# A two-layer transformer kernel: a place in SBUF for every expert block's weights, loads issued from the last heads, clears in 23 pieces

## The reference, cut to what matters

```python
x = _layernorm(x + _L0_attn_ref(x, ...))   # 16 heads of 8, causal
x = _layernorm(x + _L0_ffn_ref(x, ...))    # 8 experts, top 2, 128 -> 256 -> 128, relu
x = _layernorm(x + _L1_attn_ref(x, ...))   # 16 heads of 8, causal, low-rank q and k
x = _layernorm(x + _L1_ffn_ref(x, ...))    # attention with 16 heads of 4, then 8 experts, top 2, gelu

def _L0_ffn_ref(x, Wr, br, W1, b1, W2, b2):
    logits = xf @ Wr + br
    topk_w, topk_idx = jax.lax.top_k(logits, TOP_K)
    topk_w = jax.nn.softmax(topk_w, axis=-1)
    gate = jnp.sum(jax.nn.one_hot(topk_idx, NUM_EXPERTS) * topk_w[..., None], axis=1)
    h = jax.nn.relu(jnp.einsum('th,ehf->etf', xf, W1) + b1[:, None, :])
    y = jnp.einsum('etf,efh->eth', h, W2) + b2[:, None, :]
    out = jnp.einsum('te,eth->th', gate, y)
```

## Time and profile before

| | |
|---|---|
| median of three runs | 1288.14 us (1286.03 to 1291.64) |
| the profiled execution | 1290.43 us, of which the span of the trace is 1288.6 us |
| PE busy | 1098.4 us, 85% |
| DVE, ACT, POOL busy | 69%, 58%, 26% |
| granted clock of PE, mean | 0.943 |
| stage 0's block units, stage 1's | from about 341 to 392 us, and 1162 to 1215 us |

### The profile page before, as it was taken

One profiled execution on the slowest core, in us unless ns is written; L12 is line 12 of the kernel. 1 busy time (PEld: TensorE's weight loads), 2 busy tenths in 40 slices (PEclk: granted clock), 3 DMA queues, 4 the chain that ended last, 5 costly groups with the idle time before them and its releaser, 6 DMA issues.

```text
span 1288.6 us, 25320 instructions
## 1 busy us (share of the span) xinstructions
PE 1098.4 (85%) x8672; PEld 598.6 (46%) x8672; DVE 883.8 (69%) x2110; ACT 742.8 (58%) x1535; POOL 338.9 (26%) x873
## 2 busy tenths in 40 slices
PE   5979999998659979999988998887888788866796
PEld 3456666554557645666645632212122211125675
DVE  2867767784213658888777888988998889801265
ACT  4456665566214425776656657777887667854232
POOL 8233322336204313433223310111110014200040
PEclk9899999999779979999999989999999989987898
DMA  3464333111342061234211311101111001033310
GB/s 89 116 184 105 99 91 94 36 39 52 105 125 64 19 161 39 62 94 104 74 59 41 69 34 25 25 11 27 34 34 33 17 15 32 18 90 103 93 40 25
DMA packets 73437, 83.04 MB, mean 64 GB/s; under 512 B 12406, under 2 KB 47430, under 8 KB 73054
## 3 DMA queue, kind: packets, MB, share of 16 engines
q1 hardware_dynamic: 71262, 77.22, 23.4%
q0 software_dynamic: 2048, 4.20, 1.1%
HBM read 47.98 MB, written 32.77 MB: 63 GB/s over the span
## 4 chain that ended last, share of the span: by engine, by line
PE 56%; DVE 23%; issue 7%; SPq 5%; ACT 5%; DMA 3%; POOL 1%; POOLq 0%; ACTq 0%; DVEq 0%
DVE tile_max L1132 17%; PE bank L1519 14%; PE bank L1475 11%; PE bank L1490 7%; PE bank L1688 6%; PE bank L1672 4%; ACT probs L1024 3%; PE bank L1470 3%; DMA q_parts<-x_blocks 2%; PE bank L1529 1%; PE bank L1596 1%; SPq L616 1%; SPq L617 1%; DVE tile_max L1126 1%; DVE x L1199 1%
## 5 line engine op out<-in xcount | busy, mean ns | idle before, releaser
L1024 ACT ACTIVATE probs<-bank 128x512 f32<-128x512 f32 x1088 | 576.3, 603 | 286.9 <-PE bank L1490 285.5
L1132 DVE TENSOR_REDUCE tile_max<-bank 128x1 f32<-128x512 f32 (+3 forms) x1152 | 611.8, 591 | 57.1 <-PE bank L1475 52.6
L1475 PE MATMUL bank<-qk 125*128 125x128 bf16 (+2 forms) x1664 | 397.1, 316 | 71.2 <-DVE tile_max L1132 66.6
L1490 PE MATMUL bank<-qk 128*128 128x128 bf16 (+1 forms) x1664 | 389.2, 311 | 3.9 <-ACT probs L1024 3.7
L1519 PE MATMUL bank<-probs,v_head 128*32 128x512 f32 (+3 forms) x3328 | 311.3, 463 | 0.8 <-POOL probs L877 0.7
L1475 PEld LDWEIGHTS bank<-qk 125*128 125x128 bf16 (+1 forms) x1664 | 135.4, 98 | 341.2 <-DVE tile_max L1132 258.1
L1519 PEld LDWEIGHTS bank<-probs,v_head 128*32 128x32 f32 x3328 | 142.4, 110 | 53.3 <-issue 28.0
L1490 PEld LDWEIGHTS bank<-qk 128*128 128x128 bf16 (+1 forms) x1664 | 135.6, 97 | 54.2 <-ACT probs L1024 17.1
L1126 DVE TENSOR_REDUCE tile_max<-bank 128x4 f32<-128x512 f32 x128 | 87.3, 687 | 98.1 <-PE bank L1475 97.7
L877 POOL TENSOR_SCALAR_AFFINE_SELECT probs<-probs 128x512 f32<-128x512 f32 x128 | 81.4, 636 | 141.1 <-ACT probs L1024 140.9
L845 POOL CAST neg_parts<-neg_max 128x8 bf16<-128x8 f32 x96 | 18.2, 189 | 327.1 <-DVE neg_max L1139 327.1
(11 more groups left out here) (175 smaller groups left out, 874.1 us busy)
## 6 DMA issues: line engine op xcount, KB each, us to landing
qk<-qk_parts SPq DMA_DIRECT2D x160, 144.0 KB
sb_w<-in_w SPq DMA_DIRECT2D x92, 128.0 KB, 2.5
qk_parts<-q_parts SPq DMA_DIRECT2D x48, 192.0 KB, 2.4
qk_parts<-k_parts SPq DMA_DIRECT2D x48, 192.0 KB, 3.0
x_blocks<-zeros SPq DMA_DIRECT2D x2, 1472.0 KB, 8.0
q_parts<-x_blocks SPq DMA_DIRECT2D x10, 256.0 KB, 3.5
y_blocks<-sums SPq DMA_DIRECT2D x10, 256.0 KB, 2.9
qk_parts<-q_parts SPq DMA_DIRECT2D x24, 96.0 KB, 2.3
```

The lines of the kernel that those rows point to most:

```text
L1024: nc.scalar.activation(probs[:, hd.probs_place(c), :], S2[i % len(S2)][:], ACT.Exp, scale=hd.a.scale).then_inc(sem("probs"), 1)
L1132: ins = nc.vector.tensor_reduce(tile_max[:, hd.slot, t, which:which + 1], s1[:, at:at + P * count], AX.X, ALU.max)
L1475: ins = mm(s1[:, at:at + P * count], qk[hd.query_rows, hd.place, 0, P * t:P * (t + 1)], qk[hd.query_rows, hd.place, 1, P * k0:P * (k0 + co ...
L1490: ins = mm(s2[:, at:at + P * count], qk[hd.key_rows, hd.place, 1, P * j:P * (j + 1)], qk[hd.key_rows, hd.place, 0, P * q0:P * (q0 + count) ...
```

## The change

Every block gets its own place for w1 and w2: eight in the other layer's expert storage as before, then six in the first halves of the q and k parts, four in `a_tok` and `x_plus`, five in `probs` (`block_weights`). x is given six buffers, `xgT` moves to `rest`. The weights of the first 18 blocks (`PRELOADED`) are asked for by SP inside the last heads of each run (`PRELOADS`: heads 29 to 31 with six blocks each, heads 89 to 94 with three), part ahead of `load_max`, part behind. A block's expert number is read once for both DMAs. Blocks 18 to 22 follow in `blocks`, behind all six x loads. `slots` comes one place ahead of `blocks`, with the four operations that both need moved into `ranks`. `biases` moves from the heads to the first place of the expert stage. In stage 0 the projections, norms, routing and gate sums move to other places. And each `x_blocks` is cleared by 23 DMAs of 64 KB, one per head, in place of one of 1472 KB.

```diff
+PRELOADED = 18
...
-    for i, step in zip(at, ("ranks", "blocks", "slots", "biases")):
+    for i, step in zip(at, ("ranks", "slots", "blocks")):
         put(later(place, i), (step, f))
     for i in range(TOP * TB):
-        put(later(place, at[2] + 1 + i // each), ("scatter", f, i))
+        put(later(place, at[1] + 1 + int(i / each)), ("scatter", f, i))
...
 first = at_unit(0, -1, 0)
-put_attention_out(0, 1, first, (0, 1, 2, 3, 4, 5, 6, 7, 9, 10))
-for m, i in enumerate((4, 5, 6, 8, 10, 12)):
+put(first, ("biases", 0))
+put_attention_out(0, 1, first, (0, 1, 3, 5, 6, 7, 8, 9, 11, 12))
+for m, i in enumerate((2, 4, 6, 8, 10, 12)):
     put(later(first, i), ("gx", 0, m))
...
+PRELOADS = ({29 + i: (range(6 * i, 6 * i + 3), range(6 * i + 3, 6 * i + 6)) for i in range(3)},
+            {89 + i: (range(3 * i, 3 * i + 1), range(3 * i + 1, 3 * i + 3)) for i in range(6)})
...
-        xg = [parts[0][:, i, S:T].bitcast(F32) for i in range(2)]
-        xgT = [parts[1][:, i, S:T].bitcast(F32) for i in range(2)]
+        xg = [part[:, i, S:T].bitcast(F32) for part in parts for i in range(PARTS)]
+        xgT = [rest[:, i, :] for i in range(2)]
...
-            return w_sb[f"w1_{1 - f}"], w_sb[f"w2_{1 - f}"]
+            w1, w2 = w_sb[f"w1_{1 - f}"], w_sb[f"w2_{1 - f}"]
+            at = [(w1[:, e, :], w2[:, e, :, :].rearrange("p f d -> p (f d)")) for e in range(E)]
+            wide = [part[:, i, 0:S].bitcast(F32) for part in parts for i in range(PARTS)]
+            wide += [tile[:, t:t + 4, :].rearrange("p t d -> p (t d)") for tile in (a_tok, x_plus) for t in (0, 4)]
+            wide += [probs[:, 4 + i, :] for i in range(5)]
+            return at + [(tile[:, 0:F], tile[:, F:2 * F]) for tile in wide]
...
                 if g + AHEAD + 1 < run.stop:
                     load_head(g + AHEAD + 1)
+                f = 0 if run is RUNS[0] else 1
+                preloads = PRELOADS[f].get(g, ((), ()))
+                if preloads[0]:
+                    preload(f, preloads[0])
                 if g + 1 < run.stop:
                     load_max(g + 1)
+                if preloads[1]:
+                    preload(f, preloads[1])
...
+            def load_block_weights(f, j):
+                e = nc.sync.value_load(expert_i[0:1, j:j + 1], min_val=0, max_val=E - 1)
+                w1, w2 = block_weights(f)[j]
+                sp.dma_start(w1, inp[f"w1_{f}"][0][:, bass.ds(e, 1), :].rearrange("p a f -> p (a f)")
+                             ).then_inc(sem(f"w_in{j // TPC}"), 16)
+                sp.dma_start(w2, inp[f"w2_{f}"][0][:, bass.ds(e, 1), :, :].rearrange("p a f d -> p (a f d)")
+                             ).then_inc(sem(f"w_in{j // TPC}"), 16)
+
+            def preload(f, blocks):
+
                 sp.wait_ge(sem("experts_known"), f + 1)
                 ge(sp, "y_ps", UNITS * f)
+                taken(sp, "aT", 2 * f, 1)
+                if f == 0:
+                    sp.wait_ge(sem("normed"), NORM_OF[(1, 1)])
+                elif blocks[-1] >= PRELOADED - 2:
+                    sp.wait_ge(sem("scattered"), 16 * TOP * TB * (f + 1))
+                for j in blocks:
+                    load_block_weights(f, j)
...
                 for m in range(BLOCK_UNITS):
                     n = len(blocks_of(m))
-                    if m + 2 < BLOCK_UNITS:
-                        taken(sp, "gx", f, m)
-                        load_x(f, m + 2)
-                        sp.wait_ge(sem("hid_ps"), UNITS * f + m + 1)
-                        load_w1(f, m + 2)
-                        sp.wait_ge(sem("y_ps"), UNITS * f + m + 1)
-                        load_w2(f, m + 2)
+                    sp.dma_start(xg[m][:, 0:P * n].rearrange("p (j d) -> p j d", d=D),
+                                 x_blocks[f].rearrange("(j p) d -> p j d", p=P)[:, TPC * m:TPC * m + n, :]
+                                 ).then_inc(sem(f"x_in{m}"), 16)
+                sp.wait_ge(sem("pv"), BATCHES[RUNS[f].stop])
+                for j in range(PRELOADED, BLOCKS):
+                    load_block_weights(f, j)
...
-                if g in (2, 4):
-
-                    sp.dma_start(x_blocks[g // 2 - 1].rearrange("(j p) d -> p j d", p=P),
-                                 zeros[:].unsqueeze(1).to_broadcast([P, BLOCKS, D])).then_inc(sem("cleared"), 16)
+                if g < BLOCKS:
+                    clear(0, g)
```

More of the change, by code:

```diff
@@ L184, in blocks_of @@
     return range(TPC * m, min(TPC * (m + 1), BLOCKS))
-def blocks_in(f, m):
-    mine = [len(blocks_of(i)) for i in range(m % 2, BLOCK_UNITS, 2)]
-    return f * sum(mine) + sum(mine[:m // 2 + 1])
 def dense_unit(m):
@@ L302 @@
 put_routing(0, 0, place, (0, 1, 3, 4, 5))
-put_places_of_tokens(0, place, (6, 7, 8, 9), 2)
+put_places_of_tokens(0, place, (6, 7, 8), 1.78)
 def put_next_qkv(c, place):
@@ L343 @@
 put(later(place, 3), ("mtok", 1))
-put_places_of_tokens(1, place, (12, 14, 16, 20), 1)
+put_places_of_tokens(1, place, (12, 14, 16), 1)
 first = at_unit(1, -1, 0)
+put(first, ("biases", 1))
 for m, i in enumerate((0, 1, 6, 8, 10, 12)):
@@ L628, in first_blocks @@
+            def preload(f, blocks):
                 sp.wait_ge(sem("experts_known"), f + 1)
                 ge(sp, "y_ps", UNITS * f)
-                for m in range(2):
-                    load_w1(f, m)
-                for m in range(2):
-                    load_w2(f, m)
+                taken(sp, "aT", 2 * f, 1)
[5 more added lines that the diff above has]
+                    load_block_weights(f, j)
@@ L634, in first_blocks, with blocks @@
+            def blocks(f):
                 sp.wait_ge(sem("scattered"), 16 * TOP * TB * (f + 1))
[L635 to L638 removed]
                 for m in range(BLOCK_UNITS):
                     n = len(blocks_of(m))
[L641 to L647 removed]
+                    sp.dma_start(xg[m][:, 0:P * n].rearrange("p (j d) -> p j d", d=D),
[4 more added lines that the diff above has]
+                    load_block_weights(f, j)
+                for m in range(BLOCK_UNITS):
+                    n = len(blocks_of(m))
@@ L651, in blocks, with clear @@
                                  ).then_inc(sem(f"y_stored{m % 2}"), 16)
+            def clear(f, j):
+                sp.dma_start(x_blocks[f][P * j:P * (j + 1), :], zeros[:]).then_inc(sem("cleared"), 16)
             for c in range(NCH):
@@ L683, in _ @@
                 load_weight(*piece)
-            first_blocks(0)
             blocks(0)
@@ L696, in _ @@
                 at = g - RUNS[1].start - 6
+                if 0 <= g - RUNS[1].start < BLOCKS:
+                    clear(1, g - RUNS[1].start)
                 if 0 <= at < len(later_weights):
                     load_weight(*later_weights[at])
-            first_blocks(1)
             blocks(1)
@@ L1269, in take_ranks @@
                 taken(dve, *step)
-            def block_of(f):
-                many, start, end = (counted[:, i, :] for i in range(3))
+                many, start = counted[:, 0, :], counted[:, 1, :]
                 per_expert = tables[:, 0:E, :]
@@ L1280, in block_of @@
                 link(nc.vector.reduce_sum(start, per_expert, AX.X))
+            def block_of(f):
+                many, start, end = (counted[:, i, :] for i in range(3))
                 link(nc.vector.scalar_tensor_tensor(end, many, float(P), start, ALU.mult, ALU.add))
```

42 lines of the change are left out of this document (9 added, 33 removed).

## The result

| | before | after |
|---|---|---|
| median of 4 runs, us | 1287.14 (1286.03 to 1291.64) | 1226.56 (1222.26 to 1231.95) |
| span of the profiled execution, us | 1288.6 | 1230.2 |
| its mean granted clock | 0.943 | 0.959 |

The ratio is 0.9525, 95% interval 0.948 to 0.957: 60.6 us less. The predicted median was 1235.6, the predicted span 1236.1. The profiled execution is the slowest of the four.

A forecast was written before the change was run, and what follows sets the result against it. SP's queue was taken to set the expert rounds' period, starving PE. Stage 0 -19.0, stage 1 -22.4, heads -4.6 + 1.1, clears -7.6: together -52.5, from span 1288.6 to 1236.1; forecast median 1235.6 us, range 1225 to 1254.

The forecast's parts named there:

- 2.5 us of bank waits: Stage 0's rounds: 2.5 us added for waits on the one shared bank, whose every tenant must be copied out first.
- the allowance: Stage 1's rounds: the same 2.5 us for waits on the shared bank, included in the 30.7 us predicted.
- SP's own work ends before the scatter's landing: Front of stage 0: nine blocks behind the last maxima take 13.8 us, ending before the scatter has landed.
- Head 31's maxima: End of run 0's heads: their load goes out 2.6 us late against 1.6 of slack; 1.0 to 1.1 us lost.
- the biases' 4.6 us: Heads: DVE paces them and loses the biases there, so 2.3 us won in each run, 4.6 in all.
- Rival 3: Clears don't pay: 7.6 us more, 1243, chance 0.10; by the skill's large-DMA rule 11.5 lost against before, 1255, chance 0.03.
- Rival 2: Rounds of both stages: PE stays at its lower clock level, 1.2 GHz; 17 us more, 1253; chance 0.12.
- rival 4: SP's issues block on full DMA queues, delaying maxima loads: at 3 us per DMA 77 us lost, 1312; chance 0.03.
- No gate held SP: Denies a rival: scatter or experts' table gate holds SP, first wait of 10 us stays per stage, 1255; chance 0.07.
- Rival 6: PE at full level from `up(0)`, no bank waits, nothing lost in head 31: 9 us less, 1226; chance 0.05.
- case 1: The prediction as worked out, all terms as summed: 1229 to 1242 us; chance 0.60.
- the signs: Expected in the profile after, among others: `up(0)` to `up(6)` 28 to 31 us in both stages, granted clock near 1.

The follow-up runs named there:

- experiment six: Changed kernel, but in head 30 the load of head 31's maxima goes ahead of all six blocks; ratio 0.9548.
- experiment twelve: Changed kernel, but DVE finds the blocks' experts ahead of the places again, scatters one step later at the old pace; 1227.39 us, ratio 0.953.
- experiment three: Changed kernel, but the blocks' biases are looked up in the heads again, at their places of before; ratio 0.9532.
- experiment eight: Changed kernel, but in front of stage 1 DVE copies the first two sets of x before it looks up the biases; ratio 0.9523.
- run 1: Not an experiment: within one execution, the series of heads ahead of stage 1, ending with head 95.
- run 0: Not an experiment: within one execution, the series of heads ahead of stage 0, ending with head 31.
- experiments four and one: Changed kernel both times: four asks for no weights while heads run, ratio 0.9706; one puts the two 1472 KB clears back, ratio 0.9613.
- experiment ten: The changed kernel again, unedited, on a chip where the kernel before takes 1287.96 us; 1223.38 us, ratio 0.9514.
- experiments six to nine: Besides six and eight, on the changed kernel: seven puts both projections ahead of the first x transposes, ratio 0.9542; nine joins all three edits, ratio 0.952.
- ten to twelve: Besides ten and twelve: eleven is the changed kernel with projections ahead of the first x transposes and stage 1's biases behind the copies; 1220.61 us, ratio 0.9484.

## Why the prediction was right, and where it was off

**What bounds it, and the rounds.** Right: the round was SP's, and without it the two phases fell to PE's own work. In stage 0 two terms were mis-sized. I priced a matmul at 0.124 us, a sixteenth of the length of sixteen; lengths overlap, and the four at 351.75 start 0.44 us after the four at 351.31, 0.11 each. Over 156 matmuls that is 2.0 us. And I added 2.5 us of bank waits: stage 0 has none. Against these 4.5 us the first thirty-two took 0.6 more than 3.0 and sixteen at 0.11, so 29.3 predicted stands against 25.48 measured. Behind the phase, the gate work moved there cost 1.2 us instead of 2.0. In stage 1 the allowance was used, 2.13 of it in one wait, and 30.7 stands against 30.47 and 28.39; that the sum fits there has luck in it, since its matmuls were priced too high as well.

**In front of the rounds.** Stage 0: 1.3 lost was predicted, 1.7 came. Measured from the sums of head 31, the bank's first use behind the a_tok transposes came after 6.5 us before (324.36 to 330.88) and 9.2 after (316.65 to 325.86): 2.7 late, where I said 2.3. From there `up(0)` came after 8.8 us, the predicted 9.0. Here the step "SP's own work ends before the scatter's landing" failed, by little. The last scatter began at 318.92, so with the 2.98 us of the earlier trace rows x could have gone out at 321.9. SP's last block ended at 322.7, and x went out behind it at once, 0.9 us late. The nine blocks behind the last maxima took 15.3 us, not 13.8. A flight of 3.10 us instead of 3.50 gave part of it back. In experiment six x moved with SP's blocks; in experiment twelve the scatter held it. Stage 1: 0.75 predicted, 0.9 measured, and experiments three and eight confirm that the biases are what is left of the wait.

**In the heads.** Head 31's maxima were late as said, by 1.77 and 2.00 us instead of 1.1. The 11.1 us between these loads, where 9.9 were predicted, explain that. Of the biases' 4.6 us the ledger shows 4.7 in the two slow heads of run 1 alone. But the biases begin at 1072.42, in the second of them. The first gave 1.2 us without them (12.72 against 11.49), the second 3.5. In run 0 the heads from the clears to the sums of head 31 lost 0.7 in one trace and won 2.5 in the other, around the predicted 1.2 (2.3 won less 1.1 lost); it can't be told. The row of run 1's second head shows how it could give more than DVE's 2.3 us of work. The stretches of before, and then the same head after:

```profile
1071.06:1085.31 14.25, 10.91 (x67) 2.10 (x65) 12.60 (x25) 8.88 (x17) 4.89 (x9) 0.88 0.10 30
1077.00:1081.00 4.00, 3.72 (x18) 0.59 (x16) 2.69 (x6) 1.97 (x5) 0.00 (x0) 0.57 0.00 0
```

```profile
1027.48 0.71 SPq L599 DMA_DIRECT2D qk<-neg_rows  x1
...
1049.72 0.81 SPq L599 DMA_DIRECT2D qk<-neg_rows  x1
...
1038.97:1049.72 10.75, 9.04 (x67) 1.90 (x65) 10.61 (x19) 8.56 (x17) 4.82 (x9) 1.00 0.38 115
```

Behind the biases PE waited 1.51 us for row maxima, its clock was 0.57 in the four us from 1077, and row maxima waited for slow matmuls. After, the head runs at 1.00 and takes 10.75 us instead of 14.25. That this is the biases' doing is argued from the rows, and experiment three speaks against so much. Its trace has them back in this head, which takes 12.96 us at a clock of 1.00. In the traces of experiments four and one, on the same chip and without them there, the head takes 12.23 and 13.46. From this head's load of maxima to the last load of run 1 it is 60.6 us with the biases, 58.2 and 59.1 without. So on that chip they cost 1.5 to 2.4 us, no more than the 2.3 predicted for a run.

**The clears.** Right, 7.6 against 8.0, and shown in both directions. That SP's next issue takes 4 us behind a big clear was not in the working; it is part of the same delay. Rival 3 fell, with the part of it that went by the skill's rule.

**The other rivals.** The lower clock through the rounds did not come: 0.93 and 0.87 in the rows above. Rival 2's price was worked out wrong: 1.73 x 2 x 5 x 2 is 34.6, not 17, so 1270, and it belonged with what the range leaves out, 0.25 in place of 0.13. SP's issues did not block in rival 4's sense: of the 92 weight DMAs four took 0.76 to 1.85 us to issue, all others 0.43 or less. No gate held SP. Rival 6 names the number that came, 1226, and that is chance. Of its terms only "no bank waits" came, in stage 0 alone; head 31's loss was there, and the first thirty-two matmuls took 5.4 and 5.8 us in the two stages, where 16 cost 1.8 once PE had run for a while.

**The sum.** 52.5 predicted, 58.4 between the profiles, 60.6 between the medians: +4.7 from stage 0, +2.4 from run 1's two slow heads, -1.9 from run 0's heads, the rest under 0.5 each. The 1.9 are no more than what two traces of one kernel differ by there. The 2.4 come again in experiment ten's trace, but of the 4.7 they belong to, 1.2 lie in a head without the biases. The measured 1226.56 lies in the range from 1225 to 1254, but below the 1229 to 1242 of case 1, the likeliest. Of the signs, 25.48 in stage 0 lies outside the 28 to 31, and stage 1's clock of 0.87 was not near 1. What was right is the mechanism of the rounds, the clears and the two fronts; the size was 8 to 9 us short of some 60.

## What to carry to other kernels

When one queue issues loads, stores and loads again, look at what stands behind a wait or a long list in it: here giving every load a place of its own, with the steps around it reordered, was worth some 38 us. With 46 loads in a row, the stores behind them, which have two places, cost 14 us. Before removing a wait, ask what is late next: the wait for maxima went, and the wait for x grew by more. Large transfers that nobody waits for hurt because short ones that somebody waits for stood behind them; cutting them up and spreading them won 8 to 10 us here.

## What was not expected of the hardware

The chips of these runs differ by 2% on the same program (1287.96 and 1317.56 us), and at particular places. On the chip of experiments six to nine, experiment eight's trace has a stretch in which PE does nothing for 2 us in the middle of a head and then runs at the lower clock level; three heads at the end of run 1 take 39.1 us instead of 31.1. And POOL's first norm behind the gathers waits 12.74 us:

```profile
1063.00:1065.00 2.00, 0.00 (x0) 0.00 (x0) 0.74 (x2) 0.70 (x2) 0.04 (x1) 1.00 0.40 135
1065.00:1067.00 2.00, 1.99 (x10) 0.30 (x10) 1.74 (x3) 1.36 (x3) 0.00 (x0) 0.51 0.59 182
...
400.18 0.24 POOL L796 TENSOR_SCALAR rstd<-mean_var 128x4 f32<-128x4 f32 x1 [12.74 <-DVE mean_var L1201]
```

In the changed kernel on the first chip it waits 2.40:

```profile
389.19 0.24 POOL L796 TENSOR_SCALAR rstd<-mean_var 128x4 f32<-128x4 f32 x1 [2.40 <-DVE mean_var L1201]
```

The gathers' results come some 10 us later there. The wait is 10.7 to 13.7 us in the traces of experiments three and six to nine, and 2.4 in those of ten to twelve. The kernel before takes 25 to 30 us more on these chips too, so the change has no part in it; no run here tells why.
